# A graph, attention and expert block on one core: the mixing weights' product first, the value product ahead of the contexts, splits and marks put in another order

## The reference

```
xn = layernorm(x)                                        # x: 1250 x 512
gnn:  twice  relu(segment_sum((h @ W.T + b)[src], dst))  # 20000 edges
mix:  q = softmax_rows(xn @ Wq.T) / sqrt(512);  k = softmax_columns(xn @ Wk.T);  v = xn @ Wv.T
      y = q @ (k.T @ v) + xn;   y @ W1.T @ W2.T + xn
x1 = x + gnn(xn) + mix(xn)
ffn:  gates = sinkhorn(layernorm(x1) @ gate_weight);  top 156 nodes per expert, 8 experts, scattered back
out = x1 + ffn(layernorm(x1))
```

## Time and profile before

| | |
|---|---|
| median of 3 runs | 469.77 us (468.29 to 471.64) |
| profiled execution, its own time | 468.61 us |
| its span, first to last instruction | 466.8 us |
| mean granted clock of TensorE | 0.999 |
| TensorE busy | 451.0 us, 97% |
| VectorE, ScalarE, GpSimd busy | 320.9, 150.6, 63.1 us |

### The profile page before, as it was taken

The page is one execution under the profiler, slowest core; times in us unless marked ns, Lnnn a source line. Parts: engine busy times, 40 slices in busy tenths (PEclk is TensorE's granted clock), DMA queues, the critical chain, the costliest instruction groups (busy, mean ns, idle before and its releaser), DMA issues.

```text
span 466.8 us, 6816 instructions
## 1 busy us (share of the span) xinstructions
PE 451.0 (97%) x2424; PEld 360.6 (77%) x2424; DVE 320.9 (69%) x1104; ACT 150.6 (32%) x272; POOL 63.1 (14%) x90
## 2 busy tenths in 40 slices
PE   7999999999999999999999999999999998878995
PEld 3788778888888888888779999877777776655783
DVE  6995699899998988897752110444645666777972
ACT  4686453322323332332222110222133114551110
POOL 4088200000000000000004000002300000006642
PEclk9999999999999999999999999999999999999999
DMA  8902002911000000001200000002744449305891
GB/s 219 287 1 91 1 0 91 219 50 65 2 1 1 1 1 1 1 2 20 108 0 4 1 1 1 1 0 53 277 139 134 134 142 380 131 1 190 289 356 71
DMA packets 20846, 40.46 MB, mean 87 GB/s; under 512 B 2953, under 2 KB 3283, under 8 KB 20805
## 3 DMA queue, kind: packets, MB, share of 16 engines
q1 hardware_dynamic: 18549, 32.55, 22.4%
q0 software_dynamic: 2256, 7.39, 4.5%
HBM read 30.10 MB, written 10.31 MB: 87 GB/s over the span
## 4 chain that ended last, share of the span: by engine, by line
PE 86%; DVE 8%; ACT 2%; issue 1%; DMA 1%; SPq 0%; POOLq 0%; DVEq 0%
PE ps L736 46%; PE ps L1031 9%; PE ps L957 9%; PE ps L848 5%; PE ps L723 5%; PE ps L1167 2%; ACT scrap_a L1424 1%; PE ps L1048 1%; PE ps L1137 1%; DMA X<-in_x 1%; PE ps L880 1%; PE ps L770 1%; PE ps L984 1%; PE ps L1008 1%; PE ps L1078 1%
## 5 line engine op out<-in xcount | busy, mean ns | idle before, releaser
L1713 DVE TENSOR_SCALAR RING_D<-places,PLACES 125x170 bf16<-125x170 f16 (+1 forms) x239 | 63.5, 266 | 0.0
L1714 DVE TENSOR_SCALAR RING_S<-iota,HOME 125x128 bf16<-125x128 f16 x239 | 60.4, 253 | 0.0
L957 PE MATMUL ps<-AT,H1H 125*128 125x416 f32 (+1 forms) x108 | 38.0, 352 | 0.0
L957 PE MATMUL ps<-AT,H1L 125*128 125x416 f32 (+1 forms) x108 | 38.0, 351 | 0.0
L1031 PE MATMUL ps<-H2H,AT 125*125 125x512 f32 x90 | 36.1, 402 | 0.0
L1031 PE MATMUL ps<-H2L,AT 125*125 125x512 f32 x90 | 35.5, 394 | 0.0
L1048 PE MATMUL ps<-WE0H 128*128 128x512 f32 x129 | 35.4, 408 | 0.0
L1781 DVE TENSOR_TENSOR ps<-ps,bias 125x512 f32<-125x512 f32 x20 | 14.0, 700 | 27.9 <-PE ps L736 27.9
L1860 DVE SCALAR_TENSOR_TENSOR ZL<-ps,ZH 128x416 fp32r<-128x416 f32 (+1 forms) x12 | 6.3, 585 | 38.7 <-ACT ZH L1369 38.7
L723 PEld LDWEIGHTS ps<-RING_D,RING_S 125*125 125x125 bf16 x239 | 25.7, 136 | 7.9
L605 POOL TENSOR_TENSOR G2L<-RAW_G,G2H 128x512 fp32r<-128x512 f32 x4 | 5.0, 1287 | 192.2 <-ACT G2H L1186 192.2
(11 more groups left out here) (410 smaller groups left out, 1171.7 us busy)
## 6 DMA issues: line engine op xcount, KB each, us to landing
RAW_E<-in_experts SPq DMA_DIRECT2D x8, 1024.0 KB, 9.9
RAW_AGAIN<-in_experts SPq DMA_DIRECT2D x3, 1024.0 KB
X<-in_x SPq DMA_DIRECT2D x1, 2240.0 KB
out_x<-X SPq DMA_DIRECT2D x10, 224.0 KB
scratch<-X SPq DMA_DIRECT2D x10, 224.0 KB
scratch<-Y SPq DMA_DIRECT2D x10, 224.0 KB
RAW_K<-in_WkT SPq DMA_DIRECT2D x4, 256.0 KB, 4.2
RAW<-in_mW2T SPq DMA_DIRECT2D x1, 1024.0 KB, 11.8
```

The costliest lines, as they stand in the source:

```text
L957: pe.matmul(place(f), h[0:TT, k, 128 * f:128 * (f + 1)], AT[0:TT, k, c0:c1], start=(k == 0 and n == 0), stop=False)
L1713: V.tensor_scalar(hot_d(v, width(b)), places[0:ET, 0:width(b)], PLACES[0:ET, c:c + 1], None, ALU.is_equal)
L1714: V.tensor_scalar(hot_s(v), iota[0:ET, :], HOME[0:ET, c:c + 1], None, ALU.is_equal).then_inc(done["marked"], 1)
```

## The change

mp is computed first of all, chunk of rows by chunk of rows into four banks (2, 3, 6, 7), with one load per chunk of W1 and W2 and their high and low parts made in that order; the turning of tile 0 lies before its last chunk. The gate's sums leave the start: a column of ones beside tile 0's transposed values gives them in `quads`. vp takes mp's place behind the k products. The last two contexts are done bank by bank, `ks` follows, and cp runs with the row chunk outside and the four banks inside. Wq's splits move from cp's stage into the contexts, Wv's into the k products. `row_keys` moves behind the third tile's low part. The visits of vp go to h, 5 in each of its tiles instead of 3, marked one step earlier. Areas of memory are moved so that this fits.

```diff
+MIX_BANKS, VALUE_BANKS = (2, 3, 6, 7), (6, 7, 0, 1)
...
-WARM, WARMER = 12, 8
+WARM = 9
...
-            use(f"xt{i}", high, ("xth_ready", i + 1), ("xtl_ready", i + 1))
-
+            use(f"xt{i}", (4, 5) if i < 4 else high, ("xth_ready", i + 1), ("xtl_ready", i + 1))
+
+    for c, b in enumerate(MIX_BANKS):
+        use(f"mp{c}", (b,), ("mph_ready", c + 1), ("mpl_ready", c + 1))
...
-        use(f"mp{c}", (4, 5, 6), ("mph_ready", c + 1), ("mpl_ready", c + 1))
+        use(f"vp{c}", (4, 5, 6), ("vph_ready", c + 1), ("vpl_ready", c + 1))
...
-    for c in range(C):
-        use(f"vp{c}", (6, 7), ("vph_ready", c + 1), ("vpl_ready", c + 1))
-        if c == 0:
-            use("ks", (5,), ("krs_ready", 1))
-    for c in range(C):
-        use(f"cp{c}", low, ("cph_ready", c + 1), ("cpl_ready", c + 1))
+    use("ks", (5,), ("krs_ready", 1))
+    for c, b in enumerate(VALUE_BANKS):
+        use(f"cp{c}", (b,), ("cph_ready", c + 1), ("cpl_ready", c + 1))
...
-    spots = [("vp0", 6, 3)]
-    for u in ("vp1", "vp2", "vp3", "cp0", "cp1", "cp2", "cp3"):
-        spots += [(u, n, 3) for n in (0, 6)]
+    spots = [("cp", n, 3) for n in range(0, 48, 6)]
...
-    spots += [(f"h{i}", 6, 3) for i in range(NT)]
+    for i in range(NT - 1):
+        spots += [(f"h{i}", 0, 2), (f"h{i}", 6, 3)]
...
         WVH, WVL = pair("WV", [128, C, D], 141)
-        WQH, WQL = pair("WQ", [128, C, D], 173)
-        G1H, G1L = pair("G1", [128, C, D], 173)
+        WQH, WQL = pair("WQ", [128, C, D], 141)
...
-        chunks = [(n, c) for n in splits for c in range(C)]
-        by_dve = [("wk", 0), ("wk", 3), ("w1", 1), ("w1", 3)] + [(n, c) for n in ("wv", "wq", "g1") for c in range(C)]
+        chunks = [(n, c) for c in range(C) for n in ("w1", "w2")] + [(n, c) for n in ("wk", "wv", "wq", "g1", "g2") for c in range(C)]
+        by_dve = [("w1", c) for c in range(C)] + [("wk", 0), ("wk", 3), ("wv", 1), ("wv", 3)] + [(n, c) for n in ("wq", "g1") for c in range(C)]
...
+            def load_pair(c):
+                f = slice(128 * c, 128 * (c + 1))
+                sp.dma_start(RAW_A[:, c, :], mW1[f, :]).then_inc(ld_pair[c] if c else loads["first_w1"], 16)
+                sp.dma_start(RAW_2[:, c, :], mW2T[f, :]).then_inc(ld_pair[c], 16)
...
+            load_pair(0)
+            load_pair(1)
             load_x(0)
+            load_pair(2)
+            load_x(1)
+            load_pair(3)
             load_wk(0)
             load_wk(1)
-            load_x(1)
-            sp.dma_start(gw1[:], rows(gate_w[0])).then_inc(loads["gate1"], 16)
             load_wk(2)
             load_wk(3)
             for part in range(2, len(PARTS)):
                 load_x(part)
             sp.dma_start(ROWS[0:TP], rows_in).then_inc(loads["edges"], 16)
-            load_weight("w2", mW2T)
-            load_weight("w1", mW1)
             for last, name, w in (("w1", "wv", Wv), ("wv", "wq", WqT), ("wq", "g1", gW1T)):
...
+            for c in range(C):
+                split_lo("w2", c)
...
-            for c in range(C):
-                split_lo("w2", c)
-            split_lo("w1", 0)
-            split_lo("w1", 2)
+            split_lo("wv", 0)
+            split_lo("wv", 2)
             for i in range(4, NT):
                 rest_of_x(i)
-            reads(pool, f"mp{C - 1}")
+            reads(pool, f"k{NT - 1}")
+            pool.wait_ge(done["xnl_ready"], NT)
...
+            link(nc.gpsimd.memset(YT[:, 0, :, TT:TT + 1], 1.0))
...
-            pe.wait_ge(done["consts"], 1)
...
+            def mix_weights(c, f, a, b, first=False, last=False):
+                w = ((W1H, W1L)[a], (W2H, W2L)[b])
+                return pe.matmul(PS[plan[f"mp{f}"][0]][:], w[0][:, c, 128 * f:128 * (f + 1)], w[1][:, c, :], start=first, stop=last)
+
+            for c in range(C - 1):
+                pe.wait_ge(*hi_of("w2", c))
+                for f in range(C):
+                    mix_weights(c, f, 0, 0, first=(c == 0))
+                pe.wait_ge(*lo_of("w1", c))
+                for f in range(C):
+                    mix_weights(c, f, 1, 0)
+                pe.wait_ge(*lo_of("w2", c))
+                for f in range(C):
+                    mix_weights(c, f, 0, 1)
+            pe.wait_ge(done["consts"], 1)
             turn_x(0)
-            pe.wait_ge(loads["gate1"], 16)
-            ps = opens("gsums")
-            for c in range(C):
-                mm = pe.matmul(ps[0:TT, 0:NE], ones[:, 0:TT], gw1[:, c, :], start=(c == 0), stop=(c == C - 1))
-            closes("gsums", mm)
-            warm(WARMER - 4)
+            pe.wait_ge(*hi_of("w2", C - 1))
+            for f in range(C):
+                mix_weights(C - 1, f, 0, 0)
+                pe.matmul(PS[plan[f"mp{f}"][0]][:, 128 * f:128 * (f + 1)], ident[:], ident[:], start=False, stop=False)
+            pe.wait_ge(*lo_of("w1", C - 1))
+            pe.wait_ge(*lo_of("w2", C - 1))
+            for f in range(C):
+                mix_weights(C - 1, f, 1, 0)
+                closes(f"mp{f}", mix_weights(C - 1, f, 0, 1, last=True))
...
-                inside = {0: (1, 4), 1: (2, 4), 2: (3, 5), 4: (5, 3)}.get(i)
+                inside = {0: (1, 4), 1: (2, 5), 2: (3, 5), 4: (5, 3)}.get(i)
...
+            def turn_peaks():
+                pe.wait_ge(done["kmax_step"], NT)
+                opens("kmt")
+                for f in range(C):
+                    mm = pe.transpose(view("kmt")[:, f, 0:TT], KMAX[0:TT, 128 * f:128 * (f + 1)], ident[0:TT, 0:TT])
+                closes("kmt", mm)
...
             for c in range(C):
-                pe.wait_ge(*lo_of("w2", c))
-                pe.wait_ge(*lo_of("w1", c))
+                pe.wait_ge(*lo_of("wv", c))
+            pe.wait_ge(done["mpl_ready"], C)
             for c in range(C):
...
-                product(f"mp{c}", ps[:], (block_of(W1H, c), block_of(W1L, c)), (rows_of(W2H), rows_of(W2L)), before=add_one,
-                        between=peak_rows if c == 1 else None, at=8)
...
+                product(f"vp{c}", opens(f"vp{c}")[:], (block_of(WVH, c), block_of(WVL, c)), (rows_of(MPH), rows_of(MPL)),
+                        between=(turn_peaks, peak_rows, None, None)[c], at=(9, 11, 1, 1)[c])
...
+            for i in range(NT - 2):
                 for c in range(C):
-                    ps = opens(f"tt{c}") if i == 0 else PS[plan[f"tt{c}"][0]]
...
+                    context(i, c)
...
-                if i == NT - 2:
-                    pe.wait_ge(done["tiles_step"], 4)
-                    closes("flag", pe.matmul(opens("flag")[0:1, 0:1], over[0:TP, 0:1], ones[0:TP, 0:1], start=True, stop=True))
-
-            pe.wait_ge(*lo_of("wv", C - 1))
+            pe.wait_ge(done["tiles_step"], 4)
+            closes("flag", pe.matmul(opens("flag")[0:1, 0:1], over[0:TP, 0:1], ones[0:TP, 0:1], start=True, stop=True))
             for c in range(C):
...
+                for i in (NT - 2, NT - 1):
+                    context(i, c)
+
+            pe.wait_ge(done["esum_step"], NT)
+            ps = opens("ks")
+            for f in range(C):
+                mm = pe.matmul(ps[:, f:f + 1], ESUM[0:TT, 128 * f:128 * (f + 1)], ones[0:TT, 0:1], start=True, stop=True)
+            closes("ks", mm)
...
+            pe.wait_ge(done["vpl_ready"], C)
+            n = 0
             for c in range(C):
-                product(f"cp{c}", opens(f"cp{c}")[:], (block_of(TH, c), block_of(TL, c)), (rows_of(VPH), rows_of(VPL)),
-                        before=vp_ready if c == 0 else None, unit=f"cp{c}")
+                pe.wait_ge(done["tl_ready"], c + 1)
+                for f in range(C):
+                    ps = opens(f"cp{f}") if c == 0 else PS[plan[f"cp{f}"][0]]
+                    for k, (t, v) in enumerate(((TH, VPH), (TH, VPL), (TL, VPH))):
+                        visits("cp", n)
+                        n += 1
+                        mm = pe.matmul(ps[:], t[:, c, 128 * f:128 * (f + 1)], v[:, c, :], start=(c == 0 and k == 0),
+                                       stop=(c == C - 1 and k == 2))
+                    if c == C - 1:
+                        closes(f"cp{f}", mm)
             pe.wait_ge(*lo_of("wq", C - 1))
...
+                w = TT + (i == 0)
+                if i == 1:
+                    pe.matmul(ps[0:TT, SLOT:SLOT + NE], LQ[:, 0, TT:TT + 1].broadcast_to([128, TT]), fold[:], start=True, stop=True,
+                              skip_group_check=True)
...
+            for c in range(C):
+                split_hi("w1", c)
+                split_hi("w2", c)
+                if c in (1, 2):
+                    root(c - 1)
             split_hi("wk", 0)
             split_hi("wk", 1)
             turned_x(0)
-            root(1)
             split_hi("wk", 2)
+            store_mix(0)
             split_hi("wk", 3)
+            root(2)
             turned_x(1)
-            root(2)
+            store_mix(1)
+            store_mix(2)
             store_k(0)
+            store_mix(3)
...
-            split_hi("w2", 0)
-            split_hi("w2", 1)
+            split_hi("wv", 0)
```

(82 more changed lines are left out.)

106 lines of the change are left out of this document (38 added, 68 removed).

## The result

The changed kernel is slower: 470.67 us (median of 22 runs, 470.18 to 471.25) against 468.17 for the kernel before on the same chips (22 runs). The ratio is 1.0046, with a 95% interval of 1.0033 to 1.0058, so plus 2.2 us (1.5 to 2.7; 2.5 between the two medians). I had forecast 1.9 us less. The profiled execution has a span of 468.6 us against 466.8: plus 1.8.

A forecast was written before the change was run, and what follows sets the result against it. TensorE's queue was taken as the bound (busy 451.0 of 466.8 us). Terms -13.1 + 9.05 + 0.3 + 1.75 + 0.1 = -1.9 us gave a forecast of 467.9 us, range 464.0 to 471.6.

The forecast's parts named there:

- the slot behind the contexts: Between contexts and cp: vp leaves its 13.92 us slot, only ks stays (0.85 with its wait), so 13.1 us are gone.
- k products: Stage from k1 to the end of k: the forecast's sum had no term for it, so no change in length.
- rival 2: k products: VectorE sets the pace and contention lengthens the full stage by about 3.5 us, giving 471.4 us; chance 0.15.
- Middle and contexts: vp in mp's slot, then contexts following VectorE: context 4 starts 25.7 us behind k instead of 25.4, plus 0.3.
- The middle's part: Slot between k products and contexts: identity matmuls (0.55) and the wait for diag (0.33) leave it, 0.9 us less.
- The eight groups of visits stay in cp, so it is as long as before.: cp, now product by rows: keeps its eight groups of visits and its length, no change.
- My third rival: Behind cp: context_left(0) stands behind marks while q0 needs cp0's bank; a slip of 1 to 2 us gives 469.4; chance 0.1.
- Visits in h: h tiles: 44 visits where 23 were, nine groups of two at 0.18 plus the last group's extra, 1.75 us more.
- The loop over q and x: Loop between cp and h: the forecast's sum had no term for it, so no change.
- The start: Up to k1, with mp now before k0: k1 between 21.3 and 23.6, middle 22.45, so 9.05 us later.
- To the end: Behind h: the gate's sums move into quads as one short matmul, 0.1 us more.

The follow-up runs named there:

- Run 5: Changed kernel with VectorE's k-stage order as in the kernel before (tile 7 statistics before x_left(4), normalise(4) before peak(1)); 470.41 us, ratio 1.0048.
- Run 10: The ninth, with GpSimd waiting before its last three low parts of x until VectorE's first shift is done; 464.61 us, ratio 0.9917.
- the ninth: Changed kernel with edge keys back, cp by columns, wk3 rounded before mp0 is stored, the k stage's old order, G1 rounded early; 465.88 us, ratio 0.9946.
- run 2: Changed kernel with cp column by column again, its first bank waiting for each total as it comes; 470.32 us, ratio 1.0031.
- run 4: Changed kernel with the five visits of an h tile in one group instead of two and three; 470.93 us, ratio 1.0039.
- run 7: Kernel of run 2 with ScalarE rounding G1's four chunks ahead of the last copy of counts; 469.14 us, ratio 1.0014.
- run 3: Changed kernel with ScalarE rounding Wk's last chunk before it stores mp's first bank; 470.09 us, ratio 1.0023.
- run 6: Changed kernel with edge keys back, plus GpSimd waiting for diag before its last three low parts of x; 470.3 us, ratio 1.0048.

## Why the prediction was wrong

The direction was wrong, and the size by 4.1 us (1.9 less forecast, 2.2 more measured; 3.7 between the spans). The two large terms held: `k1` 9.19 us later (9.05 forecast), the slot behind the contexts 12.90 shorter (13.1). What failed are terms that I set to nothing or nearly so; with the small ones they make up the 3.7.

- *k products, forecast 0, measured +1.09.* I priced rival 2 as a full VectorE that contention makes slower and gave it 3.5 us. VectorE was no busier than before: of the 28.9 us that I added up for it, the four low parts of mp came (2.7), but tile 2's statistics and XF fell ahead of `k1`, and two splits of weights took 1.9 instead of 2.8. What failed is the order. The change itself had put tile 4's low part ahead of the statistics of tile 7, and a peak ahead of the scaling of tile 5, so that XF of tile 5 stood too late in VectorE's queue. Run 5 puts both pairs back as they were before and takes 0.93 of the 1.09 away, with the low parts of mp still in the stage. The right question was what stands ahead of each tile's XF, not whether the busy times sum to the stage.
- *Middle and contexts, forecast +0.3, measured +1.04.* The middle's part (12.09 us) was right to 0.2. The sequence of VectorE that I counted forward was right in its order, but the diag in it was counted at the 1.5 us of before, and took 2.26. GpSimd's low parts of x end 5.2 us behind the end of k in both kernels; diag moved 0.9 us forward and so lies wholly beside them. The kernel before, then the changed one (its diag is at 55.66):

```profile
39.10 8.07 POOL L611 TENSOR_TENSOR XNL<-XF,XNH 125x512 fp32r<-125x512 f32 x6
46.33 1.51 DVE L1651 TENSOR_SCALAR diag<-ident,kmt 128x128 fp32r<-128x128 f32 x4
```

```profile
53.66 3.78 POOL L615 TENSOR_TENSOR XNL<-XF,XNH 125x512 fp32r<-125x512 f32 x3 [0.26 <-ACT XNH L1211]
```

The low part of tile 2's exponential came 1.4 us earlier against the end of k, where I had 1.9. Run 10, which takes GpSimd out of the way, gives 1.40 us back against the ninth. I knew of the contention and had looked for it at the start alone. That `row_keys` would cost more than it gave was seen (1.2); it cost 1.3 us. (The forecast counts five contexts from 67.35 to context 8. They are four, and its 79.2 us is worked out with four.)

- *"The eight groups of visits stay in cp, so it is as long as before."* cp is (13.23 us, 13.22 before). But four banks that fill together also close together, within its last 3 us: the copies and low parts that used to be spread over 13 us come between 108.1 and 112.9, across cp's end at 110.4 and in front of `q0`'s maximum. +1.02 us, all of it given back by run 2. My third rival had the place and the price nearly right (VectorE behind cp, 1 to 2 us) and the wrong victim: it is not `q0`'s bank but the marks for `q1` and the softmax of tile 0.
- *Visits in h, forecast 1.75, measured 2.11.* The visits came out as priced: a tile of h takes 3.22 us where it took 3.05, so the second group costs the 0.18 that I had for it, though split otherwise (a visit 0.08, a break 0.02 to 0.03, run 4). The 0.34 us too much lie behind the last matmul of h. From its start to the first matmul of the aggregation it was 0.23 us, and is 0.57:

```profile
250.50 0.43 PE L978 MATMUL ps<-AT,H1H 125*128 125x416 f32 x1 [0.18 <-issue]
```

Between the two the kernel has TensorE's queue wait for the last copy of counts and load a flag for a branch. That copy, which follows the last visits, now ends 0.8 us before the last matmul of h starts, and 3.6 before it in the kernel before (249.2 and 249.93; 244.5 and 248.06). No run tests that this is the reason.

- *The loop over q and x, forecast 0, measured +0.66.* I hadn't looked at it. The new division of visits moves the end of each counted block, and ScalarE's rounding of G1 stood behind one (run 7 took 0.56 away; the other 0.1 is h's first group of visits).
- *The start, forecast 9.05, measured 9.19*: right by luck. The forecast took the middle between loads at two rates, 260 and 238 GB/s or 377. The loads ran between them (313 GB/s up to 12 us, 284 up to 18) and were not what set `k1`. ScalarE held a loaded chunk behind a wait for mp's first bank (run 3: 1.07 us). The number agreed, its reason did not.
- *To the end, forecast +0.1, measured -0.4*: open. The same stretch takes 218.1 to 218.8 us in the profiles of the twelve runs, and no edit touches it.

The terms for work (visits, matmuls at the faster pitch, the slot) were good to 0.2 us; the four that failed by 0.6 or more were all places in a queue, one of them with GpSimd beside it. With five orders mended and GpSimd's low parts placed, the same change gives 3.9 us less than before (468.1 x 0.0083; 3.5 between the medians).

## What to carry to other kernels

A product moved ahead pulls its copies, low parts and loads with it into other engines' queues, and each of them stands in front of something that was on time; a busy share (VectorE's was 83% of the k stage) says nothing about that. List for each moved step the next instruction behind it that TensorE waits for, on each engine, and count its due time, not the load. Three of the five mended orders (edge keys, cp by columns, the k stage) are in the main those of the kernel before: read your own diff for every step that changed places, and give each a term, if only a zero with its reason. Accumulating several banks at once saves a wait for the inputs and bunches the work on the outputs: check who needs VectorE at that moment.

## What the runs showed of the hardware

VectorE beside GpSimd pays by the instruction, and small ones pay most: an operation of 80x74 took 0.91 to 1.25 us instead of 0.24 to 0.29, about as long as one of GpSimd's low parts (3.80 us for three in run 10), a scaling of 128x128 took 0.57 instead of 0.22, one of 125x512 with two operands in SBUF 1.37 instead of 0.69, while those that read PSUM kept their 0.68. The Trainium skill (Trainium Architecture — The Big Picture, section What this means for kernel authors) calls the port pair of the two engines an exclusive lock and not a split of bandwidth. The Trainium skill (GPSIMD Engine Reference, section Key points) names instructions with two SBUF inputs or in a 2-port mode. The traces fit both: in run 6 the three small steps last 0.91, 1.25 and 1.17 us while GpSimd's low parts run, and the next one, behind their end, 0.29. That diag and `below`, with one tensor input each, pay too would fit the 2-port mode; no run tells it apart.

TensorE's first four matmuls of mp ran at twice the later pitch (0.45 us against 0.23), behind nine warming ones. In run 7, with the same nine and nearly the same start (5.52), all four together took 1.11 us instead of 1.81, and in run 10 1.49: the faster pitch sets in at another time in each execution. The granted clock reads 1.00 in this stretch in all three, so that this is the rise from 1.2 to 2.4 GHz is inferred from the pitch alone.
